# Row sums of q squared for the norm of q: from a TensorE product with ones to VectorE turns and a small product

## The reference: what is computed

```python
def _rmsnorm(x, w):
    xf = x.astype(jnp.float32)
    var = jnp.mean(xf * xf, axis=-1, keepdims=True)
    return (xf * jax.lax.rsqrt(var + EPS)).astype(x.dtype) * w
q = _rmsnorm(q, q_norm_w)
scores = jnp.einsum("bhqd,bhkd->bhqk", q, k) * scale
probs = softmax(scores + mask)
out = einsum("bhqk,bhkd->bhqd", probs, v) @ Wo.T
```

## Time and profile before

| what | value |
|---|---|
| median of 3 runs | 1418.65 us (1417.75 to 1419.18) |
| span of the profiled execution | 1417.8 us |
| TensorE busy | 1405.3 us, 99% of the span |
| VectorE, ScalarE, GpSimd busy | 850.8, 514.2, 359.5 us |

### The profile page before, as it was taken

One profiled execution on the slowest core, in us unless ns is written; L12 is line 12 of the kernel. 1 busy time (PEld: TensorE's weight loads), 2 busy tenths in 40 slices (PEclk: granted clock), 3 DMA queues, 4 the chain that ended last, 5 costly groups with the idle time before them and its releaser, 6 DMA issues.

```text
span 1417.8 us, 26787 instructions
## 1 busy us (share of the span) xinstructions
PE 1405.3 (99%) x9135; PEld 1124.3 (79%) x9136; DVE 850.8 (60%) x1807; ACT 514.2 (36%) x1117; POOL 359.5 (25%) x374
## 2 busy tenths in 40 slices
PE   9999999999999999999999999999999999999998
PEld 7888887778787787878787878787878888777777
DVE  6444447666666666666666666565678746243359
ACT  5333344333343334333333333333334331222242
POOL 1122223121212121211112121212122101366646
PEclk9999999999999999999999999999999999999999
DMA  7544331111111111111111111111123244554548
GB/s 224 180 124 141 126 116 42 38 35 38 42 37 34 38 41 39 34 37 41 39 33 43 38 41 31 47 32 42 45 79 97 97 149 164 192 194 163 162 149 297
DMA packets 91230, 125.48 MB, mean 89 GB/s; under 512 B 7184, under 2 KB 57360, under 8 KB 90896
## 3 DMA queue, kind: packets, MB, share of 16 engines
q1 hardware_dynamic: 83632, 99.70, 22.3%
q0 software_dynamic: 7520, 24.65, 5.2%
HBM read 86.84 MB, written 37.49 MB: 88 GB/s over the span
## 4 chain that ended last, share of the span: by engine, by line
PE 80%; DVE 2%; issue 1%; DMA 0%; ACT 0%; POOL 0%; DVEq 0%; ACTq 0%
PE ps L592 19%; PE ps L594 18%; PE ps L593 18%; PE ps L978 6%; PE ps L679 5%; PE ps L721 4%; PE ps L994 3%; PE ps L687 2%; PE ps L706 2%; PE ps L973 1%; DVE acc L1878 1%; DVE acc L1885 1%; PE ps L1025 1%; PE ps L891 1%; PE ps L729 0%
## 5 line engine op out<-in xcount | busy, mean ns | idle before, releaser
L489 POOL CAST vth<-vt 128x256 fp32r<-128x256 f32 x64 | 25.4, 396 | 629.6 <-PE ps L721 618.0
L1483 DVE TENSOR_TENSOR al<-ps,ah 128x256 fp32r<-128x256 f32 x256 | 96.0, 417 | 116.3 <-ACT ah L1165 116.3
L1165 ACT CAST ah<-ps 128x256 fp32r<-128x256 f32 x256 | 83.6, 384 | 194.8 <-PE ps L594 188.4
L1477 DVE TENSOR_TENSOR acc<-ps,acc 128x512 f32 (+1 forms) x128 | 87.9, 687 | 109.0 <-PE ps L594 109.0
L592 PE MATMUL ps<-hT,w0h 128*128 128x512 f32 (+1 forms) x384 | 152.2, 396 | 0.0
L594 PE MATMUL ps<-hT,w0h 128*128 128x512 f32 (+1 forms) x384 | 149.9, 390 | 0.0
L593 PE MATMUL ps<-hT,w0l 128*128 128x512 f32 (+1 forms) x384 | 149.5, 389 | 0.0
L483 POOL TENSOR_TENSOR qr<-qv,mhalf 128x8 f32<-128x8 f32 x64 | 105.1, 1642 | 83.4 <-DVE qv L1492 82.3
L1134 ACT COPY qs<-ps 128x512 f32<-128x512 f32 x128 | 75.2, 587 | 120.9 <-PE ps L594 120.9
L1143 ACT ACTIVATE pb<-pb 128x256 f32<-128x256 f32 x128 | 48.3, 418 | 166.3 <-DVE pb L1510 166.2
L592 PE MATMUL ps<-w0l,ah 128*128 128x512 f32 x256 | 103.0, 402 | 0.0
(11 more groups left out here) (238 smaller groups left out, 3079.0 us busy)
## 6 DMA issues: line engine op xcount, KB each, us to landing
wraw<-in_w_att SPq DMA_DIRECT2D x64, 256.0 KB, 2.6
vbuf<-vo SPq DMA_DIRECT2D x16, 512.0 KB, 3.3
kbuf<-ko SPq DMA_DIRECT2D x16, 512.0 KB, 3.8
kt<-kbuf SPq DMA_DIRECT2D x32, 256.0 KB, 2.9
vt<-vbuf SPq DMA_DIRECT2D x64, 128.0 KB, 2.0
wgu<-in_w_gu SPq DMA_DIRECT2D x4, 2048.0 KB, 8.1
y<-ybuf SPq DMA_DIRECT2D x16, 512.0 KB, 6.2
xt<-in_x SPq DMA_DIRECT2D x16, 256.0 KB, 4.0
```

The costliest lines, as they stand in the source:

```text
L1165: act.copy(ah[:, bp, :, b2, :], pv_view(bp, b2)).then_inc(a_hi, 1)
L1477: dve.tensor_tensor(dst, PS[6 + bp][:], dst, ALU.add).then_inc(acc_done, 1)
L1483: dve.tensor_tensor(al[:, bp, :, b2, :], pv_view(bp, b2), ah[:, bp, :, b2, :], ALU.subtract).then_inc(a_lo, 1)
```

## The change

In all steps but the first three and the last seven, the sums leave TensorE but for one small product. VectorE turns the squares of a head of q in 32x32 blocks (`turn_squares`, 512 columns from SBUF to SBUF) and sums each turned block along its columns (`sum_squares`). This gives, on each partition, 16 sums for each of the two heads: four bands of 32 partitions hold the four quarter sums of the same rows. `split_sums` rounds these 32 numbers to fp32r and puts what is left over beside them, 64 columns in all. TensorE multiplies them with `fold`, a 128x128 matrix of zeros and ones in fp32r that adds the four bands and gives each of them the result (`add_quarters`). VectorE reads the 64 columns, adds half the epsilon to each of the two parts, keeps on each partition the numbers that belong to its rows (`quarters` is one or zero), and sums to `qv`.

The small product stands between the heads 1 and 2 of `project_out(1)`. VectorE's order changes too: the turns and sums of the next step's squares stand in front of `a_rest(i-1, 0)`, `probs_lo(i)` of an even step stands in front of the softmax instead of inside it, and `slice_lo` of an even step moves into the next odd step, between the sum of the first head and the turn of the second. ScalarE's `squares` now wait until VectorE has turned the last ones. `fold` is prepared in the first stage, `quarters` in the opening of the attention; the SBUF places of some tiles move.

```diff
+TURNED = (3, STEPS - NC)
...
+        def turned(j):
+            return not isinstance(j, int) or TURNED[0] <= j < TURNED[1]
...
+            def add_quarters(j):
+                pe.wait_ge(sq_part, j - TURNED[0] + 1)
+                pe.matmul(PS[2][:, 0:64], fold[:].rearrange("p a j -> p (a j)"),
+                          sqs_hl[:].rearrange("p x n -> p (x n)"), start=True, stop=True).then_inc(ss_done, 1)
...
-            def outputs(r, w_before, w_o, o_ready=None):
+            def outputs(r, w_before, w_o, o_ready=None, turn=True):
                 pe.wait_ge(acc_done, 2 * r + 1)
-                project_out(1, w_before, (0, 1, 2, 3))
+                project_out(1, w_before, (0, 1))
+                if turn:
+                    add_quarters(r + 2)
+                project_out(1, w_before, (2, 3))
...
                 scores(d + odd, 1 - odd)
-                q_sums(i + 1)
+                if not turn:
+                    q_sums(i + 1)
...
             def squares(h, j):
-                act.wait_ge(ss_done, j + 1)
+                if not isinstance(j, int) or turned(j - 1):
+                    act.wait_ge(sq_turned, 2 * (j - 1 - TURNED[0]) + h + 1)
+                else:
+                    act.wait_ge(ss_done, j + 1)
...
+            def turn_squares(j, h):
...
+                dve.wait_ge(q_sq, 2 * j + 1 + h)
+                dve.transpose(sqT[:].rearrange("p n i -> p (n i)"), sq[:, h].rearrange("p b s -> p (b s)")).then_inc(
+                    sq_turned, 1)
+
+            def sum_squares(j, h):
+                dve.wait_ge(sq_turned, 2 * (j - TURNED[0]) + h + 1)
+                dve.tensor_reduce(sqs[:, h].rearrange("p r b -> p b r"),
+                                  sqT[:].rearrange("p (b r) i -> p b r i", r=2), AX, ALU.add).then_inc(sq_sums, 1)
+
+            def split_sums(j):
...
+                dve.tensor_copy(sqs_hl[:, 0, :], flat).then_inc(sq_sums, 1)
+                dve.wait_ge(sq_sums, k + 3)
+                dve.tensor_tensor(sqs_hl[:, 1, :], flat, sqs_hl[:, 0, :], ALU.subtract).then_inc(sq_part, 1)
...
             def softmax(j, *meanwhile):
...
+                    dve.scalar_tensor_tensor(out=ssg[:].rearrange("p b q -> p q b"),
+                                             in0=PS[2][:, 0:64].rearrange("p (q b) -> p q b", q=8),
+                                             scalar=HD * EPS / 2, in1=quarters[:],
+                                             op0=ALU.add, op1=ALU.mult).then_inc(ss_turned, 1)
+                    dve.wait_ge(ss_turned, j + 1)
+                    dve.tensor_reduce(qv[:], ssg[:], AX, ALU.add).then_inc(q_var, 1)
...
+                if turn:
+                    turn_squares(i + 1, 0)
                 if odd:
                     probs_lo(i, 1)
+                if turn:
+                    sum_squares(i + 1, 0)
+                    if odd:
+                        slice_lo(i - 1, w, sl - 1)
+                    turn_squares(i + 1, 1)
+                    sum_squares(i + 1, 1)
+                    split_sums(i + 1)
...
                 a_rest(i - 1, 0)
...
+                if turn and not odd:
+                    probs_lo(i, 0)
...
                 softmax(i + 1, while_root, while_exp)
-                slice_lo(i, w, sl)
+                if odd or not turn:
+                    slice_lo(i, w, sl)
```

More of the change, by code:

```diff
@@ L157, in build @@
             pb = sb("pb", [P, 8, S], F32, a)
-            sst = sb("sst", [P, 8, 32], F32, a)
+            ssg = sb("ssg", [P, 8, 8], F32, a)
+            quarters = sb("quarters", [P, 8, 8], F32, a)
+            sqs = sb("sqs", [P, 2, 2, 8], F32, a)
+            sqs_hl = sb("sqs_hl", [P, 2, 32], F32R, a)
+            ones32 = sb("ones32", [P, 32], F32, a)
             v_hi = sb("vth", [P, 2, HD], F32R, a)
@@ L211, in build @@
             g_hl = sb("g_hl", [P, KD, P], F32R, a)
+            sqT = sb("sqT", [P, 16, 32], F32, a)
+        with ExitStack() as a:
+            sb("below_sst", [P, KD * P], F32, a)
+            sst = sb("sst", [P, 8, 32], F32, a)
         with ExitStack() as a:
@@ L220, in build @@
         rab = sb("rab", [P, NT, E], BF16)
+        fold1 = sb("fold1", [P, 32])
+        fold = sb("fold", [P, 4, 32], F32R)
+        quarter = sb("quarter", [P, 4])
         xt3 = (sgt[0], aft[0])
@@ L245, in build @@
         ss_turned, v_split, pT_hi = sem("ss_turned"), sem("v_split"), sem("pT_hi")
+        sq_turned, sq_part, fold_ok = sem("sq_turned"), sem("sq_part"), sem("fold_ok")
+        sq_sums = sem("sq_sums")
         pT_done, pT_evac, pv_done, a_hi, a_lo, o_done, acc_done = (
@@ L750, in outputs, with step @@
                 project_out(0, w_o, (0, 1, 2, 3))
-            def step(d, odd, pair_q, w_q, w_before, w_o, q_ready=None, o_ready=None, last=False):
+            def step(d, odd, pair_q, w_q, w_before, w_o, q_ready=None, o_ready=None, last=False, turn=True):
                 i = 2 * d + odd
@@ L780, in step @@
                     transpose_probs(i, odd)
-                outputs(i - 1, w_before, w_o, o_ready)
+                outputs(i - 1, w_before, w_o, o_ready, turn)
             for k in range(KD):
@@ L820, in opening @@
                 scores(1, 1)
-                q_sums(3)
+                pe.wait_ge(fold_ok, 5)
                 pe.wait_ge(acc_done, 4)
@@ L831, in group @@
                 else:
-                    step(d0, 0, 0, W[p], W[1 - p], W[1 - p])
-                    step(d0, 1, 1, W[p], W[1 - p], W[p], o_ready=i0 + 8)
+                    step(d0, 0, 0, W[p], W[1 - p], W[1 - p], turn=not last)
+                    step(d0, 1, 1, W[p], W[1 - p], W[p], o_ready=i0 + 8, turn=not last)
                 with pe.Fori(1 if first else 0, NC // 2 - 2) as t:
-                    step(d0 + 1 + t, 0, t + 1, W[p], W[p], W[p])
-                    step(d0 + 1 + t, 1, t + 2, W[p], W[p], W[p])
-                step(d0 + NC // 2 - 1, 0, NC // 2 - 1, W[p], W[p], W[p], last=last)
+                    step(d0 + 1 + t, 0, t + 1, W[p], W[p], W[p], turn=not last)
+                    step(d0 + 1 + t, 1, t + 2, W[p], W[p], W[p], turn=not last)
+                step(d0 + NC // 2 - 1, 0, NC // 2 - 1, W[p], W[p], W[p], last=last, turn=not last)
                 if not last:
@@ L1467, in _ @@
                         kv_tile(2 * m + cp, 4 * m + 2 * cp + tt, cp, tt)
+            dve.wait_ge(ident_ok, 2)
+            dve.tensor_reduce(fold1[:], ident[:].rearrange("p (a j) -> p j a", a=4), AX, ALU.add).then_inc(fold_ok, 1)
+            dve.tensor_reduce(quarter[:], ident[:].rearrange("p (a j) -> p a j", a=4), AX, ALU.add).then_inc(fold_ok, 1)
+            dve.wait_ge(fold_ok, 2)
+            dve.tensor_copy(fold[:], fold1[:].unsqueeze(1).to_broadcast([P, 4, 32])).then_inc(fold_ok, 2)
             for n in range(NT - 4, NT):
@@ L1484, in a_rest @@
                                       ALU.subtract).then_inc(a_lo, 1)
+            def turn_squares(j, h):
+                k = 3 * (j - TURNED[0]) + h
+                if not isinstance(k, int) or k > 0:
+                    dve.wait_ge(sq_sums, k)
+                dve.wait_ge(q_sq, 2 * j + 1 + h)
[6 more added lines that the diff above has]
+            def split_sums(j):
+                k = 3 * (j - TURNED[0])
+                flat = sqs[:].rearrange("p h r b -> p (h r b)")
+                dve.wait_ge(sq_sums, k + 2)
+                dve.tensor_copy(sqs_hl[:, 0, :], flat).then_inc(sq_sums, 1)
+                dve.wait_ge(sq_sums, k + 3)
+                dve.tensor_tensor(sqs_hl[:, 1, :], flat, sqs_hl[:, 0, :], ALU.subtract).then_inc(sq_part, 1)
             def softmax(j, *meanwhile):
@@ L1488, in softmax @@
                 dve.wait_ge(ss_done, j + 2)
-                dve.transpose(sst[:].rearrange("p b r -> p (b r)"), PS[2][:, 0:256]).then_inc(ss_turned, 1)
-                dve.wait_ge(ss_turned, j + 1)
-                dve.tensor_scalar(qv[:], sst[:, :, 0], HD * EPS, None, ALU.add).then_inc(q_var, 1)
+                if not turned(j):
+                    dve.transpose(sst[:].rearrange("p b r -> p (b r)"), PS[2][:, 0:256]).then_inc(ss_turned, 1)
+                    dve.wait_ge(ss_turned, j + 1)
+                    dve.tensor_scalar(qv[:], sst[:, :, 0], HD * EPS, None, ALU.add).then_inc(q_var, 1)
+                else:
+                    if j is TURNED[0]:
+                        dve.wait_ge(fold_ok, 5)
+                    dve.scalar_tensor_tensor(out=ssg[:].rearrange("p b q -> p q b"),
+                                             in0=PS[2][:, 0:64].rearrange("p (q b) -> p q b", q=8),
+                                             scalar=HD * EPS / 2, in1=quarters[:],
+                                             op0=ALU.add, op1=ALU.mult).then_inc(ss_turned, 1)
+                    dve.wait_ge(ss_turned, j + 1)
+                    dve.tensor_reduce(qv[:], ssg[:], AX, ALU.add).then_inc(q_var, 1)
                 half = lambda t, hp: t[:, CB * hp:CB * hp + CB, :]
@@ L1543, in residual, with dve_step @@
                 dve.bn_stats(st, row).then_inc(st_done, 1)
```

(20 more changed lines are left out.)

1 line of the change is left out of this document (removed).

## The result

The changed kernel takes 1397.28 us (median of 4 runs, 1396.35 to 1398.59), the kernel before 1418.2 beside it (1417.18 to 1419.18): a ratio of 0.9855, 95% interval 0.9841 to 0.9869, or 20.9 us. Forecast were 1395.4 us and a gain of 23.3 us.

A forecast was written before the change was run, and what follows sets the result against it. TensorE's slots were taken to bound the attention steps. The profiled span 1417.8, less 23.8 for 54 steps, plus 0.5 for preparation and opening, gave 1394.5, or 1395.4 us against the median; range 1389 to 1408.

The forecast's parts named there:

- The bound: In the attention steps TensorE never waits, so the time is the sum of its slots from start to start.
- The slot removed: `q_sums` behind the scores on TensorE: 0.57 us a step, bounds 0.48 (a shape change stays) and 0.57.
- The slot added: The small product between projection matmuls on TensorE: 0.13 us, between 0.034 and 0.32, a little over the turns' 0.10.
- The count: 54 turned steps (j = 3 to 56), each gaining 0.57 less 0.13: 23.8 us.
- preparation and opening: Four small operations preparing fold and quarters, plus the opening of the attention: 0.5 us added (0 to 1).
- VectorE's prices: Turn of 512 columns 0.71 us (0.69 to 0.90), half's sum 0.69, split two times 0.18, product's read and sum 0.23 each.
- The third rival: VectorE's turn of squares at half the pace per column, 1.42 us, makes the kernel slower: 1429.1 us; chance 0.06.
- The odd delivery: In odd steps `sq_part` is ready at 623.92, TensorE comes at 624.24: 0.24 us to spare with the wake-up off.
- The even delivery: In even steps, through GpSimd's root, scale and probabilities: 0.30 us in all before TensorE waits at the probabilities' turns.
- The second rival: Odd step's delivery late as `slice_lo` meets GpSimd's split of v: 1405, or 1410; chance 0.18 including a 0.32 product slot.
- The first half's 1.43: VectorE's turn and sum of the first half of squares, 1.43 us, fit its 2.39 us idle in an even step.
- The point of reference: Profiled span 1417.8 us taken as equal to the fastest run, with the median of three runs 0.85 above it.

The follow-up runs named there:

- e1: The changed kernel with the small product issued twice in each of the 54 turned steps: 1404.55 us.
- e2: The changed kernel with the four products with ones put back on TensorE in 53 turned steps, into columns nobody reads: 1427.18 us.
- e3: The changed kernel with one more unused VectorE sum over 512 columns ahead of the split, in odd steps alone: 1411.36 us.
- e4: The changed kernel with one more unused VectorE sum over 512 columns behind the split, in even steps alone: 1405.6 us.
- e6: The changed kernel with the outer loops of both VectorE and TensorE written out: 1394.66 us, ratio to the kernel before 0.9838.

## Why the prediction was right, point by point

- **The bound.** TensorE's slots set the time: e1 and e2 move it by 0.12 and 0.56 a slot.
- **The slot removed** was forecast at 0.57 and is 0.56 by e2; the lower bound of 0.48, with a change of shape that stays, is out.
- **The slot added** was forecast at 0.13 and is 0.12 by e1 and by the timeline. The turns of the probabilities, 0.10, were the right neighbour. By the 25 ns that the Trainium skill ("TensorE: Matmul & The Clock Gate", Back-to-back issue gap) gives for an isolated matmul, 29 us would have been won. The slot of the product alone is indeed 0.03, but the matmul behind it pays for its weights.
- **The count** was 54 steps at 0.44, 23.8 us. Measured are 53 at 0.43, 23.0: in the opening, the first turned step gives nothing, which the 0.5 us for preparation and opening cover.
- **VectorE's prices.** The turn was put at 0.71 by slope, and is 0.71. The third rival, half the pace, falls with it. The read of the product was put at 0.23 and takes 0.28.
- **The odd delivery** was given 0.24 us of room; e3 shows 0.22.
- **The even delivery** was given 0.30; e4 shows 0.58 or more. The estimate was too tight because the root ends earlier against the scale than I had it: 0.42 us before it in the changed kernel, where 0.20 with the wake-up was forecast.
- **The second rival**, the collision with GpSimd's split, does not occur: `slice_lo` ends 0.1 before it. Nothing here tests the rule on who goes first.
- **What was missed** is the jumps, which cost 3.1 us and for which the sum has no term; its only loss is the 0.5 us for "preparation and opening". The step that failed is the count: "The loops turn 54 steps" takes the steps behind the two jumps like all others. There "The first half's 1.43 falls into idle time: 2.39 us in an even step" does not hold: VectorE's next instruction comes 2.7 to 3.0 us behind its branch, and in the kernel before it came after 0.24. And `a_rest`, for which I checked only the matmul that asks for it, also sets how early TensorE gets past its last wait in front of the jump, and so whether its slow branch is covered.
- **The point of reference.** A run's time is about 1.7 us above the span of its profile (1397.51 and 1395.8 in the profiled run), so the profiled execution, with its span of 1417.8, was not at the fastest run, as the sum took it, but nearer to 1419.5. Since the gain was taken off the median, this does not move the forecast.

## What to carry to other kernels

Where TensorE never waits, price a change by the slots from start to start, the added matmul together with the weights of the next one, and then look for the deliveries; a small matmul in a stream of wide ones costs 0.12 us here, not its columns. A jump back of a long loop can be covered and cost nothing: TensorE's takes over 3 us in both kernels here, and shows once the last wait in front of it is met later. VectorE's was quick before and slow with the changed code. Look at the jumps apart from the ordinary steps, and write out an outer loop of a few rounds when both engines pay for it.

## What the runs showed of the hardware that was not expected

- TensorE's branch back to the head of the long outer loop lasts 3.28 to 3.75 us with one instruction packet behind its start (16 jumps) and 4.70 to 5.01 with two (8 jumps), in the old code and the new. Its last wait in front of the jump met 3.8 us or more ahead of its last matmul, the gap is 0.07 at most; at 3.0 to 3.7 it is 0.27 to 2.3. The branches of the inner loops, of two steps, last 0.25 at most.
- VectorE's branch there is followed by its next instruction after 2.7 to 3.0 us in the changed kernel and its edits (16 jumps), and after 0.24 in the kernel before and its edits (8 jumps). Written out, the loops have neither loss (e6).
- A scratch tile of 32 bytes in front of the projection's operands goes with projection matmuls of 396 ns instead of 389, 0.2 us in a pair of steps. The cause was not tried alone.
